# Where ScalarE reads the small products of an attention step: between the second and third exponential of the next step, with a normalisation in halves and a row of maxima moved up in the queue

## What is computed

```python
# layer 0, per image: hidden_states is x, 128 x 1024
x = group_norm(hidden_states, pre_g, pre_b) + pos_emb
s1 = silu(conv2d(x, sa_w1, 1x1)); s2 = silu(conv2d(s1, sa_w2, 3x3))
spatial_enhanced = x * sigmoid(conv2d(s2, sa_w3, 1x1))
sh = group_norm(x, norm_g, norm_b)            # "xh" in the kernel
# 8 heads of 16 over 1024 tokens, all from sh
standard_out = softmax(q k^T / 4) v
# 2 heads of 64: queries from spatial_enhanced, keys and values from sh
multi_out = [softmax(qm km^T / 8) vm, ...]
final = out(ff2(silu(ff1([standard_out, multi_out]))))
x = group_norm(final, post_g, post_b) + hidden_states
# layer 1, on the tokens of x
t = t + attention(layer_norm(t), w_qkv)       # 8 heads of 16
t = t + top-2-of-8 expert FFN(layer_norm(t))
```

## Time and profile before

| what | value |
|---|---|
| median of 3 runs | 3018.26 us (3012.58 to 3019.98) |
| the profiled execution | 3020.56 us, of which the trace spans 3018.8 us |
| TensorE busy | 2588.5 us (86%) |
| VectorE busy | 2057.8 us (68%) |
| ScalarE busy | 1783.0 us (59%) |
| GpSimd busy | 657.9 us (22%) |
| mean granted TensorE clock | 0.95 of full speed |

### The profile page before, as it was taken

One profiled execution on the slowest core, in us unless ns is written; L12 is line 12 of the kernel. 1 busy time (PEld: TensorE's weight loads), 2 busy tenths in 40 slices (PEclk: granted clock), 3 DMA queues, 4 the chain that ended last, 5 costly groups with the idle time before them and its releaser, 6 DMA issues. The chain is left out here.

```text
span 3018.8 us, 42335 instructions
## 1 busy us (share of the span) xinstructions
PE 2588.5 (86%) x15054; PEld 1029.8 (34%) x15061; DVE 2057.8 (68%) x3120; ACT 1783.0 (59%) x3502; POOL 657.9 (22%) x611
## 2 busy tenths in 40 slices
PE   3796899988989899998999889898999989998844
PEld 1122222362225322262223522253222722235234
DVE  4756878477875878667785768758786677857520
ACT  1562577556765577556775567655775567755713
POOL 4000122015120240203320151202402043202123
PEclk9997899999999999999999989999999989999957
DMA  4002220274014530164202740145301632037034
GB/s 115 2 1 49 53 33 14 88 187 75 8 52 134 115 71 1 57 193 84 38 15 92 183 77 5 57 132 111 71 1 57 198 83 34 16 99 177 11 99 137
DMA packets 171978, 228.25 MB, mean 76 GB/s; under 512 B 29680, under 2 KB 101520, under 8 KB 171664
## 3 DMA queue, kind: packets, MB, share of 16 engines
q1 hardware_dynamic: 163600, 208.90, 28.4%
q0 software_dynamic: 8192, 16.79, 2.0%
HBM read 173.39 MB, written 51.31 MB: 74 GB/s over the span
## 5 line engine op out<-in xcount | busy, mean ns | idle before, releaser
L1433 DVE TENSOR_REDUCE blockmax<-ps 128x2 f32<-128x1024 f32 x1152 | 1355.0, 1220 | 380.1 <-PE ps L787 317.2
L1249 ACT ACTIVATE prob<-ps 128x512 f32<-128x512 f32 x2048 | 1110.7, 596 | 464.9 <-PE ps L964 453.2
L964 PE MATMUL ps<-qs,ks 99*128 99x512 bf16 x2048 | 687.2, 396 | 110.6 <-ACT prob L1249 48.5
L964 PEld LDWEIGHTS ps<-qs,ks 99*128 99x128 bf16 x2048 | 177.8, 99 | 775.0 <-ACT prob L1249 641.7
L624 POOL TENSOR_TENSOR rs<-vn,vec 128x1 f32<-128x1 f32 (+1 forms) x40 | 40.2, 1005 | 1475.1 <-DVE vn L1378 1051.2
L1297 ACT ACTIVATE prob<-ps,b1t 128x128 f32<-128x128 f32 x736 | 209.7, 368 | 169.3 <-PE ps L1080 169.3
L980 PE MATMUL ps<-prob,va_b 128*32 128x512 f32 x1984 | 283.8, 646 | 1.1 <-ACT oatt L1241 1.1
L980 PE MATMUL ps<-prob,va_a 128*32 128x512 f32 x2048 | 275.7, 610 | 3.0 <-ACT oatt L1241 1.7
L1275 ACT ACTIVATE prob<-ps 128x1024 f32<-128x1024 f32 x128 | 130.2, 1023 | 160.3 <-PE ps L1037 92.8
L675 POOL DMA_INDIRECT x_dram<-ta,slot_u x128 | 124.6, 973 | 313.5 <-DVE slot_u L1653 276.9
L1033 PE MATMUL ps<-routed,km 64*128 64x512 f32 x512 | 146.8, 651 | 12.6 <-DMA mrow<-maxrow 12.6
(11 more groups left out here) (247 smaller groups left out, 3182.6 us busy)
## 6 DMA issues: line engine op xcount, KB each, us to landing
parts_dram<-parts SPq DMA_DIRECT2D x32, 768.0 KB, 4.3
ks<-parts_dram SPq DMA_DIRECT2D x192, 128.0 KB, 4.4
qs<-parts_dram SPq DMA_DIRECT2D x384, 64.0 KB, 4.4
shared<-in_w SPq DMA_DIRECT2D x96, 256.0 KB, 3.4
prob<-in_w SPq DMA_DIRECT2D x96, 256.0 KB, 3.3
routed<-in_w SPq DMA_DIRECT2D x80, 256.0 KB, 3.5
xe<-in_w SPq DMA_DIRECT2D x48, 256.0 KB, 3.4
oatt<-in_w SPq DMA_DIRECT2D x48, 256.0 KB, 3.2
```

What stands on the lines that cost most here:

```text
L964: pe.matmul(ps[:, SC + h % 2, :], ks[:, slot_of(a, g), h, t * P:(t + 1) * P], qs[:, slot_of(a, g), q, h, :], start=True, stop=True).then_i ...
L1249: act.activation(prob[:, n % 3, h, :], ps[:, SC + h % 2, :], ACT.Exp, scale=HD ** -0.5).then_inc(exp_done[a], 1)
L1433: dve.tensor_reduce(cells, banks, AX.X, ALU.max).then_inc(blocks_used[f], 1)
```

## The change

Three edits. The function `exps` gets a third argument and does a step's first or last two exponentials. ScalarE now does the first two of step n, then the small products of step n-1, then the last two of step n; the read of the last values (`last_taken`) at step 0 moves between the halves as well. `normalize` is split into two calls of 512 columns: the first stands between the halves of step 9, the second behind them, where before one of 1024 columns stood ahead of step 8. TensorE waits for one half at kA0 and qA0, for both at kA1 and qA1. In SyncE's queue the third set of rows of the token loop goes ahead of the parts of the next image's keys.

```diff
             if front:
+                if token:
+                    spread_max("b", 2)
                 spread_parts(0, 0)
                 spread_group(0, 0, 0)
-                if token:
-                    spread_max("b", 2)
                 spread_parts(0, 1)
...
                 elif name in ("kA0", "kA1", "qA0", "qA1"):
-                    pe.wait_ge(done["xh_a"], 1)
+                    pe.wait_ge(done["xh_a"], int(name[2]) + 1)
...
-            def normalize():
+            def normalize(h):
                 act.wait_ge(done["norm_coefs"], 1)
-                act.activation(xh[:, :], x1[:, :], ACT.Identity, bias=cb[:, :], scale=ca[:, :]).then_inc(done["xh_a"], 1)
+                act.activation(xh[:, cols(h)], x1[:, cols(h)], ACT.Identity, bias=cb[:, :], scale=ca[:, :]
+                               ).then_inc(done["xh_a"], 1)
...
-            def exps(a, n):
-                if n >= 3:
+            def exps(a, n, half):
+                if n >= 3 and half == 0:
                     act.wait_ge(pv_done[a], n - 2)
-                for h in range(GH):
+                for h in (2 * half, 2 * half + 1):
...
-                if n and n % NT == 0:
+                if n and n % NT == 0 and half == 1:
                     take_output(a, n // NT - 1)
...
                     if conv:
-                        exps(0, n)
+                        exps(0, n, 0)
                     if n == 0 and experts:
                         act.wait_ge(last_weighed, 1)
...
-                    for name in small.conv.get(n, ()):
+                    for name in small.conv.get(n - 1, ()):
                         small_product(name)
+                    if conv:
+                        exps(0, n, 1)
...
-                    if token and front and n == 8:
-                        normalize()
...
-                        exps(1, n)
+                        exps(1, n, 0)
+                    if token and front and n == 9:
+                        normalize(0)
+                    for name in small.token.get(n - 1, ()):
+                        small_product(name)
+                    if token:
+                        exps(1, n, 1)
+                    if token and front and n == 9:
+                        normalize(1)
                     for name in small.token.get(n - 2, ()):
                         if name in ("kA0", "kA1", "qA0", "qA1"):
                             second_part(name)
-                    for name in small.token.get(n, ()):
-                        small_product(name)
```

## The result

The changed kernel takes 2972.07 us (median of 4 runs, 2968.06 to 2972.36) beside 3019.12 for the kernel before (4 runs, 3012.58 to 3023.96): a ratio of 0.9842, 95% interval 0.9822 to 0.9863. It is faster by 47 us, where 85 were forecast, and lies above the upper end of the range, 2966. The profiled execution spans 2970.4 us; mean granted clock 0.957 (before 0.950).

The account below looks back on a forecast made before the run. TensorE's waits bound it: for normalisation coefficients, for rows with slow clock behind both, and for exponentials held by small-product reads. Token loops 9.8 us seven times, 69, plus convolution loops 16: 85 us, forecast 2933, range 2915 to 2966.

Parts of the forecast that it names:

- The normalisation: Token loop, steps 8 to 10: moved to step 9, wins 3.03 us idle plus 1.4 of slow clock, 4.4 per image.
- The rows: Token loop, step 16: third set queued first removes the 2.40 us wait and 2.8 of slow clock, 5.2 per image.
- The kA chain: Token loop, kA0 to qA1: waiting for VectorE to free the bank makes steps 3.77 against 3.50, losing 1.0 us per image.
- c10, c11 and the single reads behind them: Token loop: two-read products c10, c11 gain 1.0 us, c2 loses some 0.2, single-read products gain 0.4.
- The km steps: Convolution loop, km0 to qm1: two-read steps fall from 3.93 to 3.52 us, four gaps giving 1.7 per loop.
- the 16 that the sum has for the convolution loops: Convolution loops: 1.7 + 0.4 = 2.1 us each, eight times less what the first and last lack.
- 8 us of slack, of which the gain after that point, some 6, eats most: SyncE's queue, token loop: 8 us between the end of the spreading and the fourth set of rows, so no new wait.
- the stall moves on to step 24: Rival, token loop: fourth set of rows late if SyncE's queue is late, 36 us lost, 2969 us; chance 0.10.
- the clock stays low: Rival, token loop, behind the two removed waits: 1.4 + 2.8 us per image not won, 2962 us; chance 0.13.
- the reads hold the exponentials: Rival, small-product steps: moved reads delay exponentials 3 and 4 by 108 us, slower at 3065 us; chance 0.05.
- each low stretch follows an idle of 2 to 3 us: Remark on the granted clock in the traces, used against the rival that it stays low after the change.

Follow-up runs that it names:

- e4_before_psum: Kernel before the change, with the remainder of the row split kept in PSUM instead of SBUF: 3024.98 us, ratio 1.0019.
- e1_psum: Changed kernel with the remainder of the row split kept in the small products' PSUM bank instead of SBUF: 2970.2 us, ratio 0.9851.
- e2_rows_ahead: Changed kernel with the fourth set of rows queued ahead of the last group of the queries' parts: 2968.97 us, ratio 0.9843.
- s_two: Changed kernel, fourth set of rows ahead of the queries' last group, split remainder in PSUM only for turn_b_3 and turn_a0_0: 2938.52 us, ratio 0.9734.
- s_best: s_two with kA0, kA1, qA0 and qA1 taken at the end of their own step, as before the change: 2931.67 us, ratio 0.9708.
- p_norm: Kernel before with only the normalisation in halves at step 9: 2991.0 us, ratio 0.9888.
- p_reads: Kernel before with only the small products taken between the second and third exponential: 3017.55 us, ratio 0.9986.
- p_queue: Kernel before with only the third set of rows first in the queue: 3008.93 us, ratio 0.9962.
- s_oldreads: Kernel before with halved normalisation, third set of rows first and the two repairs of s_two, small products taken where they were: 2966.42 us, ratio 0.9819.

## Why the prediction was wrong

Most of its terms held. The normalisation gave 33.6 us (7 times 4.4 is 31), with the halves at 0.84 and 0.81 us. (The estimate of 0.80 by the Trainium skill, page "ScalarE: Activation LUTs", section "What ACT_TABLE_LOAD costs", comes near.) The rows gave 37.2 (7 times 5.2 is 36): 18.6 at step 15, nearly all of it the wait, and 18.5 at step 16, nearly all of it the clock. The second half belongs to the rows only as far as the wait brings the clock down, and e4_before_psum won the same 18.5 with waits of 2.24 to 2.71 us still there and the clock at 1.00 behind them. How often step 16 of before runs at the low level one profile cannot tell. The kA chain cost 7.8 (7.0 were summed): its steps last 3.79 and 3.79, against 3.77 worked out, and TensorE there waits 0.37 us for VectorE, as said. c10, c11 and the single reads behind them gave 6.9 of the 7 times 1.0 in steps 17 to 20. The km steps went from 3.93 to 3.56 (3.52 worked out); of the 16 that the sum has for the convolution loops the column shows 10.5, because step 15 ran at a mean clock of 0.65 in two of them (3.1 lost) and 1.7 of the gain lie in step 20, outside the column.

The step that failed is the one that priced what comes behind the rows: "8 us of slack, of which the gain after that point, some 6, eats most". It followed one queue, SyncE's, named GpSimd only as the maker of c2's input, and put the splits at nothing: it never asked where GpSimd would stand when TensorE is 5 us earlier. GpSimd had no slack: its chain ended 0.1 us before the split that now meets it. SyncE's slack itself was about as counted (it was free 0.8 us before the split ended), but the rows, issued right behind twelve transfers, took 7.76 us to the score and not 5.93 (e1_psum), which the sum had not allowed for. With `turn_a0_0` at the loop's end, which nothing in the sum touched, that takes 18.6 + 12.6 = 31 us of the 37 missing; most of the remainder is the convolution loops' 10.5 in place of 16.

The rival "the stall moves on to step 24" had nearly the right time (2969) with 0.10, and half the mechanism; that its number came so near is luck, for it put 36 us at step 24, where steps 20 to 25 lose 18.6 and the loop's end the rest. The rows are late at step 24, but SyncE was free at 1427.55, before the split ended at 1428.34: late were the split, held by GpSimd, and the landing behind twelve transfers of queries' parts. Neither alone is worth the loss (e1_psum, e2_rows_ahead). That the clock stays low and that the reads hold the exponentials were not seen: the clock of 1.00 behind both places speaks against the first, the shorter steps with two reads against the second.

With both causes out of the way the sum nearly comes true: s_two, which keeps all of the change, won 79 us of the 85. s_best won 86, but it has also undone the kA term, without which the sum would be 92.

Open stays why the granted clock falls behind the same wait at step 16 in most loops of before, in some of p_norm and p_reads and in none of e4_before_psum; no run took that apart. The prediction's remark that each low stretch follows an idle of 2 to 3 us holds for the two places that it read, but not throughout: in e4_before_psum such an idle had no low stretch behind it, and the low stretches of the last section have no idle of that length before them.

## What to carry to other kernels

When an edit makes one engine earlier at a place, list for every other engine what it is doing at the places behind, relative to the engine that moved: an engine at 22% busy had a stretch of 25 us with hardly a pause, and that stretch decided. Look in the profile of before for the loop in which the coincidence already happens; here one cast of 0.91 beside six of 0.21 or 0.22 showed the mechanism, though not its size. And when a repair seems worth nothing, look whether it repaired and broke something else: e1_psum won 12.5 us at the loop's end and lost as much to a bank that came free later.

## What the runs showed of the hardware

GpSimd's `conv_in` instructions use 32 partitions and the split 16, and still the one holds the other, by up to 1.1 us a time (1.39 against 0.28). In the trace of the changed kernel 23 casts and subtractions on SBUF operands are longer than usual, by 24.5 us together, and each ends 0.07 to 0.15 us behind the end of a GpSimd instruction; in e1_psum, with the remainder in PSUM, none of the 216 casts and second subtractions lasts over 0.28 us, though 45 of them lie wholly inside a GpSimd instruction. Between two GpSimd instructions that follow each other without a gap VectorE gets through with one instruction each.

The granted clock falls in some passes of the same code and not in others. In p_queue, step 15 of the convolution loops, with the same work in each, took 3.35 us in two loops and 4.89 in five. It follows the router's product of 16 narrow matmuls. The windows of one loop of either kind (PE, PEld, DVE, ACT, POOL, then granted clock): at 1.00 the step lasts 3.35; in the other it lasts 4.89 and the mean clock of the window is 0.66, with TensorE busy throughout both.

```profile
479.60:484.60 5.00, 5.00 (x21) 1.26 (x21) 3.46 (x13) 2.17 (x4) 0.00 (x0) 0.66 0.02 5
832.60:836.10 3.50, 3.50 (x22) 1.09 (x22) 2.88 (x12) 2.17 (x4) 0.00 (x0) 1.00 0.02 3
```

All seven such loops of before had 3.35 in its profile, s_oldreads had five slow ones, s_best none; so a term of 1.54 us a loop there cannot be told from such changes by one profile. What decides it, no run here shows.
